# Row maxima and splitting in the routed stage, attention in double key blocks, and every low part of the probabilities on VectorE

## The reference, cut to what matters

```
kv_latent = x @ W_to_kv.T;  c = kv_latent @ W_compress.T
ch = layernorm(c) * ln_gamma + ln_beta
q, k, v = rope(ch @ Wq.T), rope(ch @ Wk.T), ch @ Wv.T
scores = q @ k.T / sqrt(64), future keys masked
o = softmax(scores) @ v
out = (o @ W_comp2lat.T) @ W_to_kv + (o @ W_comp2lat.T) @ W_out_res.T + b_out_res
routed: g = xs @ gate_w[e]; u = xs @ up_w[e]; h = silu(g) * u; dn = h @ down_w[e]
        out[token] += weight * dn          # tokens sorted by expert
```

## Time and profile before

| | us |
|---|---|
| median of three runs | 2112.65 |
| the profiled execution: device time | 2114.9 |
| the profiled execution: span of its records | 2113.2 |
| stage `prepare` | 0 to 768 |
| stage `routed`, from the first weight load to the last matmul's result | 768 to 1532 |
| stage `attend` | 1541 to 2113 |

### The profile page before, as it was taken

One profiled execution on the slowest core, in us unless ns is written; L12 is line 12 of the kernel. 1 busy time (PEld: TensorE's weight loads), 2 busy tenths in 40 slices (PEclk: granted clock), 3 DMA queues, 4 the chain that ended last, 5 costly groups with the idle time before them and its releaser, 6 DMA issues. The chain is left out here.

```text
span 2113.2 us, 29578 instructions
## 1 busy us (share of the span) xinstructions
PE 1859.5 (88%) x8572; PEld 1450.5 (69%) x8572; DVE 1141.1 (54%) x2257; ACT 778.7 (37%) x1510; POOL 798.4 (38%) x856
## 2 busy tenths in 40 slices
PE   2899999999999969999999899999927899778997
PEld 1677777777777757777777777777715667556675
DVE  5776777767777523322222222222246788567874
ACT  2222222222222213333333333333314566745665
POOL 1544444344443413333334333333312334413343
PEclk7899999999999989999999999999958999989998
DMA  7656565655666344444444544453266654776532
GB/s 265 213 189 197 194 204 208 196 193 186 215 195 191 123 167 155 157 162 152 159 157 162 210 159 156 161 194 117 69 183 132 165 112 122 154 180 163 118 100 60
DMA packets 146998, 348.48 MB, mean 165 GB/s; under 512 B 19404, under 2 KB 41036, under 8 KB 146880
## 3 DMA queue, kind: packets, MB, share of 16 engines
q1 hardware_dynamic: 102912, 242.03, 34.4%
q0 software_dynamic: 43968, 104.91, 18.9%
HBM read 204.14 MB, written 146.67 MB: 166 GB/s over the span
## 5 line engine op out<-in xcount | busy, mean ns | idle before, releaser
L1061 POOL DMA_INDIRECT expert_rows<-res,ids_all x143 | 145.3, 1016 | 431.7 <-ACT res L1013 420.9
L1332 ACT ACTIVATE ex<-sc 128x512 f32<-128x512 f32 (+3 forms) x288 | 165.3, 574 | 161.8 <-PE sc L1238 160.5
L872 POOL DMA_INDIRECT token_list<-tok,slot x128 | 125.7, 982 | 246.3 <-DVE slot L636 210.3
L1217 PE MATMUL mb<-khl,qh 128*128 128x512 f32 (+3 forms) x288 | 116.7, 452 | 96.1 <-DVE qlm L1354 47.1
L69 PE MATMUL egu<-w,rT_0h 128*128 x576 | 189.1, 410 | 2.0 <-SPq L927 2.0
L1361 DVE TENSOR_REDUCE mx<-mb 128x1 f32<-128x512 f32 (+3 forms) x288 | 175.0, 641 | 24.3 <-PE mb L1217 20.9
L69 PE MATMUL egu<-w,rT_1h 128*128 x568 | 184.4, 406 | 0.0
L1037 DVE TENSOR_TENSOR eh<-egu,esg 128x256 f32<-128x256 f32 x143 | 60.7, 424 | 226.3 <-ACT esg L1003 226.3
L1056 POOL DMA_INDIRECT rows<-xn_scratch,rows_all x143 | 138.5, 968 | 74.1 <-issue 42.6
L1217 PEld LDWEIGHTS mb<-khl,qh 128*128 128x128 f32 x288 | 59.0, 210 | 138.5 <-DVE qlm L1354 53.4
L1003 ACT ACTIVATE esg<-egu 128x256 f32<-128x256 f32 x143 | 54.9, 384 | 232.4 <-PE egu L69 232.4
(11 more groups left out here) (284 smaller groups left out, 4826.7 us busy)
## 6 DMA issues: line engine op xcount, KB each, us to landing
w<-expert_parts SPq DMA_DIRECT2D x64, 768.0 KB, 7.8
base<-expert_rows POOLq DMA_DIRECT2D x32, 1024.0 KB, 12.4
expert_parts<-ew_h SPq DMA_DIRECT2D x32, 768.0 KB, 3.3
expert_parts<-ew_l SPq DMA_DIRECT2D x32, 768.0 KB, 5.7
x<-x SPq DMA_DIRECT2D x16, 1024.0 KB, 5.3
xn_scratch<-xn SPq DMA_DIRECT2D x16, 1024.0 KB, 5.9
base_scratch<-xb SPq DMA_DIRECT2D x16, 1024.0 KB, 5.3
base<-base_scratch SPq DMA_DIRECT2D x16, 1024.0 KB, 8.9
```

The costliest lines, as they stand in the source:

```text
L872: pool.indirect_dma_start(list_d[:, :], bass.IndirectOffsetOnAxis(ap=slot[q][:, j, c:c + 1], axis=0), tok[q][:, j, c, :], None).then_inc(s ...
L1061: pool.indirect_dma_start(parts_d[:, :], bass.IndirectOffsetOnAxis(ap=ids_all[:, t:t + 1], axis=0), res[t % 2][:, :], None, bounds_check=2 ...
L1217: mm = pe.matmul(mb[g % 2][:, 0:w], qh[n % 2][:, j * P:(j + 1) * P], khl[:, key:key + w], start=True, stop=(c < m))
L1332: i = act.activation(dst[:, off:GROUP], sc[u % NSC][:, off:GROUP], ACT.Exp, scale=SCALE)
```

## The change

The row maxima of all 16 groups are now worked out in the routed stage, about two units per tile from tile 3 to tile 137, and written once to memory (`row_maxima`); attention loads each group's row straight into `qlm`. The loading and splitting of keys and values moves there too, and `khl`, `kh1`, `vhl` and the folded matrix `mop` stay in SBUF across the stages; the folding itself and the memsets of `kh1` (now on GpSimd) stand at the routed stage's start. There `ehb` and `edb` have one bank each instead of two, which frees two for the maxima, and rows are gathered 8 tiles ahead instead of 4. Attention goes in steps: two full key blocks at once (112 steps, `sc` tiles of two banks, 1024 columns for exp and low part) and the four diagonal blocks singly (64 steps). It has two `sc` tiles, two `ex`, three probability tiles, `LAG` 2, two `ob` banks and two sets of `oT`. `by_pool` is false everywhere, so that VectorE makes each low part; GpSimd keeps the clearing and the accumulating transfers. Queries are loaded and split once more in attention.

```diff
-AHEAD = 4
+AHEAD = 8
+KEY_GROUPS = [n % QB + 1 for n in range(NG)]
+FIRST_MAX = [GT * sum(KEY_GROUPS[:n]) for n in range(NG + 1)]
+FIRST_SLOT, LAST_SLOT = 3, TILES - 6
+def maxima_until(t):
+    done = -(-FIRST_MAX[NG] * (t + 1 - FIRST_SLOT) // (LAST_SLOT + 1 - FIRST_SLOT))
+    return min(FIRST_MAX[NG], max(0, done))
 def routed(...):
-        tb, gu, hb, db = [[ps(f"e{n}{i}") for i in range(2)] for n in ("tb", "gu", "hb", "db")]
+        tb, gu, mb = [[ps(f"e{n}{i}") for i in range(2)] for n in ("tb", "gu", "mb")]
+        hb, db = ps("ehb"), ps("edb")
         # sync
+            for dst, src in ((wz, w_kv), (wo, w_outT), (wc[:, :], w_c2l), (wv[:, :], w_vT), (gam[:, :], gamma), (bet[:, :], beta),
+                             (fold[:, 0, :], fold_in), (tri[:, :], tri_in[1])):
+                sp.dma_start(dst, src).then_inc(const_in, 16)
             load(0, 0, None)
         # tensor
+            def max_scores(g):
+                n, j, c, width = unit(g)
+                if g == FIRST_MAX[n]:
+                    pe.wait_ge(highs, 4 * n + 2)
+                    pe.wait_ge(k_low, n + 1)
+                after(pe, m_red, g - 1)
+                own = c == n % QB
+                key = n // QB * T + c * GROUP
+                mm = pe.matmul(mb[g % 2][:, 0:width], qh[n % 3][:, j * P:(j + 1) * P], khl[:, key:key + width],
+                               start=True, stop=not own)
+                if own:
+                    mm = pe.matmul(mb[g % 2][:, width - P:width], identb[:, :], future[:, :], start=False, stop=True)
+                mm.then_inc(m_done, 1)
             for t in range(TILES):
+                some, others = maxima(t)
                 gate_up(t)
                 if t > 0:
                     down(t - 1)
+                for g in some:
+                    max_scores(g)
                 if t + 2 < TILES:
                     turn(t + 2)
+                for g in others:
+                    max_scores(g)
                 turn_hidden(t)
         # scalar: load_block(n) and split_high(n, which) between downed(t - 1) and hidden_turned(t)
         # vector
             for t in range(TILES):
                 hidden(t)
+                for g in some:
+                    reduce_max(g)
                 if t + 2 < TILES:
                     turned(t + 2)
+                for g in others:
+                    reduce_max(g)
+                for n, which in splits[t]:
+                    split_low(n, which)
                 hidden_turned(t)
         # gpsimd
-            for t in range(AHEAD):
+            for t in range(AHEAD - 4):
+                gather(t)
+            pool.memset(value(kh1[C:P, :]), 0.0).then_inc(blank, 1)
+            pool.wait_ge(blank, 1)
+            pool.memset(value(kh1[C:C + 1, :]), 1.0).then_inc(blank, 1)
+            for t in range(AHEAD - 4, AHEAD):
                 gather(t)
 def attend(...):
-        NE, NP, NSC = 3, 5, 3
-        LAG, NB = 3, 4
+        NE, NP, NQ, NB = 2, 3, 3, 4
+        LAG = 2
+        sc = [ps(f"sc{i}", 2) for i in range(2)]
+        ob = [ps("ob0"), ps("ob1")]
-        by_pool = [kb % 2 == 1 and GT < kb and kb < u - GT for u in units for kb in range(u)]
+            steps += [(n, kb, 2) for kb in range(0, own, 2)] + [(n, own + d, 1) for d in range(GT)]
+        by_pool = [False for _ in steps]
+        finish = {first[n + 1] - 1 + LAG: n for n in range(NG)}
+            gap = max(1, (first[n + 2] - first[n + 1]) // GT) if n + 2 <= NG else 1
+                project_at[first[n + 1] + LAG + 1 + j * gap] = (n, j)
         # tensor
+                after(pe, e_done, i - 1)
+                for c in range(count):
+                    dst, key = sc[i % 2][:, c * GROUP + to:(c + 1) * GROUP], slice(at + c * P, at + (c + 1) * P)
+                    pe.matmul(dst, khl[:, key], qh[n % NQ][:, to:GROUP], start=True, stop=False)
+                    mm = pe.matmul(dst, kh1[:, key], qlm[n % NQ][:, to:GROUP], start=False, stop=True)
+            for i in range(TAIL):
+                if i < len(steps):
+                    scores(i)
+                if LAG <= i < len(steps) + LAG:
+                    outputs(i - LAG)
+                if i in project_at:
+                    project(*project_at[i])
         # scalar
+                act.wait_ge(s_done, i + 1)
+                low_there(act, i - NE)
+                after(act, pv_done, i - NP + 1)
+                for dst in (ex[i % NE], prp[i % NP][0]):
+                    e = act.activation(dst[:, span(i)], sc[i % 2][:, span(i)], ACT.Exp, scale=SCALE)
         # sync
+            for n in range(NQ):
+                load_queries(n)
             for n in range(NB):
                 load_base(n)
```

More of the change, by code:

```diff
@@ L1019, in _ @@
                 silu(t)
+                for n in loads[t]:
+                    load_block(n)
                 if t + 2 < TILES:
@@ new lines, in attend @@
+        steps = [(n, kb, 2) for n in range(0)]
+        for n in range(NG):
+            own = GT * (n % QB)
+            steps += [(n, kb, 2) for kb in range(0, own, 2)] + [(n, own + d, 1) for d in range(GT)]
+        first = [next(i for i, (n, _, _) in enumerate(steps) if n == m) for m in range(NG)] + [len(steps)]
+        by_pool = [False for _ in steps]
+        pool_before = [sum(by_pool[:i]) for i in range(len(steps) + 1)]
+        finish = {first[n + 1] - 1 + LAG: n for n in range(NG)}
+        project_at = {}
@@ L1157, in attend @@
-        start = [1 if u == GT else 3 if u == 2 * GT else 5 for u in units]
-        def steps(n):
-            ahead = units[n + 1] if n + 1 < NG else 0
-            over = units[n] - 2 - start[n]
-            for kb in range(units[n]):
-                behind = [j for j in range(GT) if n and kb == min(1 + j * (n % QB + 1), units[n] - 1)]
-                yield kb, range(*(min(ahead, max(0, -(-ahead * k // over))) for k in (kb - start[n], kb - start[n] + 1))), behind
+            if by_pool[i]:
+                eng.wait_ge(pool_low, pool_before[i] + 1)
+            else:
+                eng.wait_ge(dve_low, i - pool_before[i] + 1)
@@ new lines, in outputs @@
+            def outputs(i):
+                n, kb, count = steps[i]
+                low_there(pe, i)
+                if i == first[n]:
+                    after(pe, o_ev, n - 1)
+                to = span(i).start
+                for c in range(count):
+                    b, at = n // QB * QB + (kb + c) // GT, slice(c * GROUP + to, (c + 1) * GROUP)
+                    for a in range(2):
+                        mm = pe.matmul(ob[n % 2][:, to:GROUP], vhl[:, b, (kb + c) % GT, :], prp[i % NP][a][:, at],
+                                       start=(kb + c == 0 and a == 0), stop=(i + 1 == first[n + 1] and a == 1))
+                mm.then_inc(pv_done, 1)
@@ L1275, in _ @@
-            pe.wait_ge(mo_ev, 2)
-            pe.matmul(pj[:, :], fold2[:, :], mo, start=True, stop=True).then_inc(mo_done, 1)
-            for n in range(NG):
-                for kb, ahead, behind in steps(n):
-                    scores(n, kb)
-                    for v in ahead:
-                        max_scores(n + 1, v)
-                    if kb >= LAG:
-                        outputs(n, kb - LAG)
-                    for j in behind:
-                        project(n - 1, j)
-                for kb in range(units[n] - LAG, units[n]):
-                    if kb == units[n] - LAG + 1 and n + 1 < NG:
-                        turn_max(n + 1)
-                    outputs(n, kb)
@@ new lines, in exps, with output_high @@
+            def exps(i):
+                act.wait_ge(s_done, i + 1)
[3 more added lines that the diff above has]
+                    e = act.activation(dst[:, span(i)], sc[i % 2][:, span(i)], ACT.Exp, scale=SCALE)
+                e.then_inc(e_done, 1)
+            def output_high(n):
+                act.wait_ge(pv_done, first[n + 1])
+                after(act, p_done, GT * (n - 1))
+                act.copy(oT[n % 2][0][:, :], ob[n % 2][:, :]).then_inc(o_hi, 1)
@@ L1340, in _ @@
+            for n in range(NQ - 1):
+                queries_high(n)
+            for i in range(TAIL):
+                if i < len(steps):
+                    exps(i)
+                    n = steps[i][0]
+                    if i == first[n] + 1 and n + NQ - 1 < NG:
+                        queries_high(n + NQ - 1)
+                if i in finish:
+                    output_high(finish[i])
         @block.vector
         def _(dve):
-            links = [0]
-            def link(i):
-                links[0] += 1
-                i.then_inc(chain, 1)
-                dve.wait_ge(chain, links[0])
@@ L1427, in _ @@
-            for j in range(GT):
-                combine(NG - 1, j)
+            for q in range(NQ):
+                i = dve.memset(value(qlm[q][C:P, :]), 0.0)
+            i.then_inc(blank, 1)
+            dve.tensor_copy(last[:, :], ident[:, C - 1:C + 1]).then_inc(ready, 1)
+            for n in range(NQ - 1):
+                queries_low(n)
```

(11 more changed lines are left out.)

479 lines of the change are left out of this document (227 added, 252 removed).

## The result

The changed kernel takes 2046.97 us (median of 4 runs, 2045.49 to 2049.86) against 2113.53 for the kernel before on the same chip: ratio 0.969, 95% interval 0.966 to 0.972. It is 3.1% faster; 1972 was forecast, a ratio of 0.933. The profiled execution has a span of 2045.4 us, 73 more than the forecast span.

What follows compares the result with a forecast made beforehand. TensorE was taken to bound the routed stage, and TensorE with VectorE's waits to hold attention. 2113.2 + 7 (start) + 24 (routed pace) - 172 (attention) = 1972 us; forecast 1940 to 2000 at 55%, whole range 1925 to 2035.

Steps and rivals of the forecast that it cites:

- Pairs 2.1 us apart: Attention: sign of a wrong forecast if full pairs of key blocks start over 2.1 us apart; 1.84 was expected.
- Start: Start of the routed stage: constants and block loads ahead of `gate_up(0)` cost +7 us, bounds +3 to +20.
- The folding and four splits on ScalarE lie beside the weights: Start of the routed stage: this work overlaps the weight transfers, so nothing was added for it to the +7 us.
- Late gathers: Routed stage: gathering 8 tiles ahead removes 32 us of waits and most of the slow clock, leaving 691 us.
- Cost of the pass on TensorE: Routed stage: the added maxima cost 60 us and the masks 8 us, all on TensorE's path, +68.
- The slack: Routed stage: `down` waiting for the hidden tile's low part, and the rest, cost 15 us, bounds 5 to 50.
- The other moves the low part by about 0.7, and the slack is about 0.6 us: Routed stage: one of VectorE's two reductions fits idle time; the second delays the hidden low part, nearly covered before `down`.
- routed stage held by VectorE's order: Rival, 8%: the hidden tile's low part is late in every tile, +35 to +50 us, 2015.
- Attention: Attention takes 19 + 346 + 12 + 7 + 16 = 400 us instead of 572.5, bounds 360 to 475.
- I add 12 us: Attention, groups 0 and 8 to 10: transfers outlast small groups; `combine` waits for the second accumulation, 12 us.
- the 21% rival: Attention, 21%: hand-overs and combines show in the pace, a pair takes 2.2 us, diagonals 4 us more: 2022.
- The memset rule: Start: by line-rate GpSimd, each `kh1` memset takes near VectorE's 6.88 us and the routed stage is 5 us shorter.

Runs made afterwards that it cites:

- both routed edits: Changed kernel, hidden tile's low part ahead of VectorE's second reduction and splits, and TensorE's table register loads ahead of `down`: 1989.44 us, ratio 0.941.
- VectorE's order changed: Changed kernel, but in the routed stage VectorE makes the hidden tile's low part ahead of the second reduction and the splits: 2017.13 us, ratio 0.955.
- start, queue and queries mended: Changed kernel, hidden low part and register loads earlier, memsets behind eight gathers, five query buffers, queries split two groups ahead: 1973.06 us, ratio 0.933.
- the counter test: Changed kernel with the low parts of 56 of the 112 full pairs on GpSimd: 2082.92 us, ratio 0.9885.

## Why the prediction was wrong

The sign and the shape were right, the size not: 73 us, of which 7.5 lie in the start, 47 in the routed pace, 1.5 in the switch of stages and 17 in attention. Of the signs named for a wrong forecast, the routed stage over 800 us is the one that came (822). Pairs 2.1 us apart did not, and `combine` waited less than 5 us in front of all its 16 first multiplications together.

**Start, +7 forecast, +14.5 measured.** The constants and the transfers came as reckoned (constants landed at 781.1). Two things failed. "The folding and four splits on ScalarE lie beside the weights": `gate_up(0)` came 13.9 us after the constants and waited last for `rT_0l`, which stands behind the folding and the splits, and not for weights. And "I take 5 us between" for the memsets as a cost of late gathers: the rows they delay were not what was late; their second memset held up an instruction of VectorE in the folding. Moving the memsets gave 3.9 us back, and the start is still +10.7.

**Late gathers, right.** They went, and the run with nothing but `AHEAD` changed gives 43 us for them. The stage without them is 707 us and not 691: "the 32 us and most of the slow clock behind them go, which leaves 691" took the whole rest of the stage for a consequence of late rows. 49.4 us of waits marked `issue` stay there for weights (140 times, at the row transposes). The matmuls themselves start later than their usual 0.23 us behind the last of `down` by 17 us in sum: the small form of what comes next, and all of the rest.

**Cost of the pass on TensorE, +68 forecast, about 71 measured.** With both routed edits no matmul behind `down` is late any more, and `down` itself starts late by 6 us in sum: 767 - 6 = 761. The kernel before with early gathers has 707 - 17 = 690. The difference of 71 is an estimate, since no run moves the register loads in the kernel before.

**The slack, 15 us forecast, some 60 measured: the step that failed.** The forecast was 691 + 68 + 15; the measured 822 us are 690, 71 and 60. Summed over the tiles from the starts of the matmuls, 44 us of the 60 lie between the last matmul of `down` and the next one, 6 in front of `down`, and most of the rest among the matmuls of the maxima. "The other moves the low part by about 0.7, and the slack is about 0.6 us" looked at the wrong event. The lead of the low part over `down` was measured rightly (0.88 before in the tile shown, 0.59 after), it even fell by less than forecast (median of all tiles 0.86 before, 0.75 after), and `down` hardly waits.

But TensorE's queue stands at the wait for the low part, and all that is behind it, six matmuls with their waits, two register loads from SBUF and the next waits, is worked off only from then on. From the end of the low part to the next weight load beyond `down` it is 2.24 us before, 2.40 after, 2.29 with VectorE's order changed (1366.21 to 1368.50), and with the loads moved ahead it was as short as 1.42. Behind the start of `down` TensorE's array has 1.13 us to the start of its last matmul (1362.33 to 1363.46). So the next weights are 0.23 us late at a lead of 0.88, 0.67 at 0.59, 0.06 at 1.10; their matmul, which can start 0.23 us after the last of `down`, is late by 0.04, 0.47 and nothing. Over all tiles of the changed kernel the medians agree: late by 0.27 us at a lead of 0.8 (47 tiles), by 0.58 at 0.2 (18 tiles), by nothing at 1.0 and above. A lead under some 0.9 to 1.0 us costs time though the wait is never seen. The kernel before had no slack left to spend.

A tile then takes the length of a loop through VectorE and ScalarE, not that of TensorE's matmuls. In the tile shown the low part ends at 1371.54; 2.40 us later come the next weights, behind them the row transposes, ScalarE's high part (1374.92), VectorE's low part of the rows, the second reduction, and the next hidden tile's low part, which ends at 1377.15, 5.61 us after the one before. Read that way, a tile is 5.6 to 5.8 us instead of 5.3.

The register loads leave no busy record; that they are the larger part is shown by moving them alone: what is lost behind `down` falls from 44 us to nothing, while 6 us more are lost in front of it, and the stage is 47 us shorter. With VectorE's order changed alone it falls to 22. The rival "routed stage held by VectorE's order" gave 2015 and named half of the mechanism; its sign, waits of `edb` for `hT_l`, showed 2.9 us by name and 10.2 marked `issue`.

**Attention, 400 forecast, 417 measured.** First scores 6.5 us in (8 forecast), first low part 17.2 in (19), pair 1.85 (1.84), exps 0.92 apart (0.92), low part 1.23 (1.24). The groups with m = 4 to 7 took in their second half 22.3, 26.1, 30.5 and 31.6 us against 23.5, 27.2, 30.9 and 34.6: all as worked out or a little better, 5.7 us there and 2 in the first half. What failed is "I add 12 us" for transfers: groups with m up to 3 took 41 us over the formula in both halves. Of its place, "where `combine` waits for the second accumulation", the runs show another: ScalarE waits 41.0 us for the row of maxima, GpSimd 83.1 for the loads and accumulations of `base`, `combine` less than 5. The comparison in the prediction, 18 us of transfers against groups of 8.7 to 16.1, was the right one; four buffers do not carry it. The transfer engines are busy for 0.84 of 167 us there, and the chain of waits shows SyncE's order: the store of 1899.86 lands, the next load of `base` is issued at 1909.77, and only behind it the queries and the row of maxima. Half the accumulations gave some 30 us back, a fifth base buffer nothing. The small loads that must come early, 2 KB of maxima per group, took 5.1 to 9.9 us in the chain of waits; queries and maxima loaded earlier gave 12.6. With start, queue and queries mended the kernel takes 1973. That this is the time forecast is chance: the forecast was for a kernel without these edits.

**Coupling, slower than before, low parts on VectorE.** ScalarE and TensorE at level pace did not disturb each other, so the 21% rival found nothing. Costing the 84 low parts that return to VectorE at nothing agrees with the pace of the pairs, 1.85 us; the counter test shows low parts on GpSimd costing some 40 us.

**The memset rule, right in length, short in effect.** The two memsets took 6.92 us each, beside 6.88 on VectorE. The Trainium skill (GPSIMD Engine Reference, Engine selection) says that one-input work on GpSimd is roughly line-rate, and these rows agree.

## What to carry to other kernels

Between two engines, the lead that counts is not the one to the first instruction that waits but to all that its queue has to work off behind the wait; here register loads from SBUF were better placed ahead of such a wait. Before a stage is shortened, its transfers are set against each single group, and the small loads that others depend on are issued well ahead of the large ones, with the step that uses them kept where it was. A change of many parts is measured by its parts: a single constant alone, in the kernel before, gave 40 of these 67 us, and moving two loads in the changed kernel gave 48 more. And when a start is compared between two traces, it is counted from the stage's own first instruction, since the stage before can differ by more than 1 us.

## What the runs showed of the hardware

An operation of GpSimd can stop one of VectorE until it ends. The scaling of 64x64 elements began at 781.73 and ended at 787.01; GpSimd's memset, which only writes, ran from 780.04 to 786.96. Without it beside, 0.24 us. Not every instruction is stopped: the addition of two 128x512 tiles at 781.12 ran beside the same memset in 0.69 us, the 0.69 of the run without it. With low parts on both engines, VectorE's ends 1.08 to 1.09 us after GpSimd's in all six meetings between 1761 and 1840 us in which VectorE began second: 1.65 us long when it began 0.56 before that end, 1.38 when it began 0.29 before, 1.23 where they do not meet. The split of the queries (64x512, line 1471) mostly took 2.48 us instead of 0.68 beside GpSimd's low parts and ended 0.54 to 0.55 after them, while `combine`, which reads PSUM, kept its 0.75 us within them.

The Trainium skill (SBUF — State Buffer, two separate sides) calls the port pair that the two engines share an exclusive lock, held for a whole instruction, and not a split of bandwidth. Both traces agree: the blocked instruction ends behind the blocker, by 0.05 us for the small one (one meeting) and by 1.08 for the large one, whatever its own start. The undisturbed addition at 781.12 and `combine` show that the lock does not meet every pair of instructions.

What stays open: the rest of the transfers' share in attention (81.9 us of waits in 11 places in the best version, which need not all be on the path), whether the bytes or the order of the transfers hold the small groups, and what the instructions behind the wait take beyond the two loads: with the loads ahead no weights were late, so the 1.42 us at the shortest lead are only an upper bound.
